# A deformable and a sign convolution on one core: the products of a tap that are added to older weights go in turn to two buffers

## The chip, the cores and the metric

One core of one Trainium2 chip. The metric is the device time of one launch in microseconds. The kernel before took 3805.28 us (median of 3 runs, 3805.22 to 3807.43). A separate, profiled execution took 3809.51 us; its profile spans 3807.5 us.

## The reference

The input `x` is 8 images of 64 x 64 pixels and 256 channels, float32. Two layers follow:

```python
x = x + L0(_gn(x))   # DCNv4: deformable, 32 groups of 8 channels, 9 taps
x = x + L1(_gn(x))   # convolution of signs, 3 x 3, scaled by means of sizes
```

Layer 0 takes the normalised image through a depthwise 3 x 3 convolution and a matmul; that gives, for each pixel, group and tap, an offset (y, x) and a mask. The value image (another matmul) is sampled at the tap's place plus the offset, by bilinear weights, multiplied by the mask and summed over the 9 taps:

```python
sampled = ((1 - ty) * (1 - tx))[..., None] * v00 + ((1 - ty) * tx)[..., None] * v01 \
        + (ty * (1 - tx))[..., None] * v10 + (ty * tx)[..., None] * v11
out = jnp.einsum('nhwgkc,nhwgk->nhwgc', sampled, mask).reshape(n, h, w, c)
return out @ op_w
```

## The kernel before, in words

**Layer 0** (`layer0`) goes through 32 steps: 8 images, and in each image 4 steps `j` = 0 to 3. A step holds 4 rows in each of 4 quarters of the image; partitions are 4 quarters x 32 groups, and the free dimension of a tile is `TOK` = 256 pixels. Image 0 and image 7 are written out, the six between them are one hardware loop, and each step is the same list of work for every engine with small additions: `j` = 2 makes the means and scales of the next image (not for the last image), `j` = 3 prepares two groups of value rows for the next image, the very last step prepares nothing.

Offsets reach less than one pixel, so each tap touches a 3 x 3 set of neighbours, and all nine taps together 5 x 5 = 25 shifts. A step therefore builds `wsum`, the weight of each of the 25 shifts (25 x 256 numbers per partition), and then multiplies the value image, shifted, by each weight and sums the 25 products.

The loop that every engine follows is over the taps `k` = 0 to 8:

- **PE** (`step`, from L838 on): `offsets` of tap k + 2 (L782) in three parts into `ps_om`, between them the first `add` of a product (L830: 16 matmuls with the identity, which turn a `pv` buffer and add it into `ps_add`), then the step's other work: `depthwise` (L753) at taps 0 to 3, `values` (L766) at 4, 5, 7, 8, `turn_back` (L795) at tap 4, `project` (L808) at taps 5 and 6; then the other adds of the tap.
- **ACT**: `hats` of tap k + 2 (L602 to L616: bilinear weights `hat` and mask `msk` from `ps_om`; it waits until the products of tap k are done, for `hat` has two buffers), then it empties PE's banks. At tap 4 (`BACK_AT`) `summed` (L623) copies the finished sums of the previous step from `ps_add` to `acc`; it stands ahead of the `hats` of tap 6 in ACT's list. `keep_back` (L631) then copies what PE turned to `acc_t`.
- **DVE** (`step`, from L1090 on): `products` of tap k (L1009), `multiply` (L1059: one shift's product over 8 channels, 128 x 2048, into one of the 4 buffers of `pv`), `add_products`, `mask_rows` for tap k + 1 (L995), and more `multiply`. There are 25 of these in a step; taps 4 and 5 have two each, the others three.
- **POOL** issues the accumulating DMAs.

Of the 9 products (3 x 3) of a tap, those at shifts that no earlier tap has touched are written to `wsum` itself; the older ones (4 or 6 planes of 256, in one or two rectangles, `tap_rects`) are first written to a buffer, `prod`, and then added to `wsum`. For taps 1, 2, 3, 6 and 7 (`SENT_TAPS`) POOL sends them by a DMA that adds (`add_products` of POOL, L479; its landing raises `wsum_added`), one after another, each behind the landing of the one before. For taps 4, 5 and 8 DVE adds them itself (L1037, `wadd_done`). Since there is one `prod`, DVE's products of tap k wait until the older ones of tap k - 1 have been added:

```python
if k > 0 and k - 1 in SENT_TAPS:
    dve.wait_ge(wsum_added, 16 * (sent_before(TAPS) * s + sent_before(k)))
```

A `multiply` waits for the landing of the last tap that touches its shift (`last_tap`), and for PE's `add` of the product that lay in its `pv` buffer before, four shifts earlier. Shift 0 is not added by PE: POOL adds it to shift 1 by a DMA (`add_pair`).

`acc` (2048 numbers per partition, as `prod`) holds the turned-out sums of the previous step from ACT's `summed` at tap 4 until PE has turned them back (`turn_back`, unit `back3`). Under the name `ahead[0]` it serves a second time: in steps `j` = 0 and 1 POOL loads half of a channel block of the next image there (`load_ahead`, L462) once `back3` is through, and ACT sums it at tap 7 (`sums_ahead`, `sums_made`).

**Layer 1** (`layer1`) is a 3 x 3 convolution of signs with its own statistics; it begins when all of layer 0 is stored and shares nothing with it but the engines.

Of the kernel before, what the change touches and what calls it, by code (L numbers as in the profile page):

```python
# [8 lines left out]
ALU = mybir.AluOpType  # L9
# [115 lines left out]
def sent_before(k):  # L125

    return sum(len(tap_rects(i // 3, i % 3)[1]) for i in SENT_TAPS if i < k)
# [75 lines left out]
def layer0(nc, x, zeros, w_dram, x2, consts, tables, mv2, reach, NI):  # L203


    with ExitStack() as ctx:
# [80 lines left out]
        ROOT_AT = 5  # L287
        BACK_AT, PROJECT_AT = 4, [5, 5, 6, 6]
        AHEAD_AT = 7

        def steps_of_images(eng, step):

# [43 lines left out]
            lo = QR * q + SR * j - 2  # L336
            return max(0, -lo), WR - max(0, lo + WR - H)

        def in_prod(rect):

            a, b, c, d = rect
            at = 6 * TOK if a == 2 and d - c == 2 else 0
            return prod[:, at:at + (b - a) * (d - c) * TOK].rearrange("p (a b t) -> p a b t", a=b - a, b=d - c)

        with nc.Block() as block:
            @block.sync
# [106 lines left out]
            @block.gpsimd  # L453
            def _(pool):
                def load_ahead(n, j, half, used):

                    src = x_v[n + 1][:, j].rearrange("p r w -> p (r w)")
                    if (n, j) != (0, 0):
                        pool.wait_ge(bg_full, unit(n, j, used, NI) + 1)
                    else:  # L460
                        pool.wait_ge(bg_full, unit(n, j, "dw3", NI) + 1)
                    nc.gpsimd.dma_start(ahead[half], src[:, HW // 2 * half:HW // 2 * (half + 1)]).then_inc(x_ahead[half], 16)  # L462

                def add_residual(n, j, units):

                    pool.wait_ge(bg_free, units)
                    for q in range(Q):
                        r0 = QR * q + SR * j
                        nc.gpsimd.dma_start(xres[:, :, q, :].rearrange("p h (r w) -> p h r w", w=W),
                                            x_v[n][:, :, r0:r0 + SR, :], accum_op=ALU.add).then_inc(xres_added, 16)  # L470

                def add_products(n, j, k):

                    s = STEPS * n + j
                    ky, kx = k // 3, k % 3
                    pool.wait_ge(prod_done, TAPS * s + k + 1)
                    at_least(pool, wsum_added, 16 * (sent_before(TAPS) * s + sent_before(k)))
                    for a, b, c, d in tap_rects(ky, kx)[1]:
                        nc.gpsimd.dma_start(wsum[:, ky + a:ky + b, kx + c:kx + d, :], in_prod((a, b, c, d)), accum_op=ALU.add)\  # L479
                            .then_inc(wsum_added, 16)  # L480

                def add_pair(n, j, uv):

                    s = STEPS * n + j
                    pool.wait_ge(pv_full, SHIFTS * s + uv + 1)
                    at_least(pool, pair_added, 16 * (len(PAIRS) * s + PAIRS.index(uv)))
                    nc.gpsimd.dma_start(pv[:, (j + uv) % PBUF, :, :], pv[:, (j + PAIRED[uv]) % PBUF, :, :],
                                        accum_op=ALU.add).then_inc(pair_added, 16)

                for n in range(NI):  # L490
                    for j in range(STEPS):
                        for k in SENT_TAPS:
                            if k == 6:
                                add_pair(n, j, 1)
                                if j < CH and n < NI - 1:
                                    load_ahead(n, j, 0, "back3")
                            add_products(n, j, k)
                        if j < CH and n < NI - 1:
                            load_ahead(n, j, 1, "project3")
                        if (n, j) != (0, 0):  # L500
                            add_residual(*previous(n, j), unit(n, j, "project3", NI) + 1)
# [15 lines left out]
            def _(act):  # L517
# [164 lines left out]
                def step(n, j, first, last):  # L682
                    s = STEPS * n + j
                    n1, j1 = following(n, j)
                    n2, j2 = following(n1, j1)
                    more = not (isinstance(n, int) and n == NI - 1 and j >= STEPS - 2)

                    def place(name):
                        return unit(n, j, name, NI), bank(n, j, name, NI)

                    for k in range(TAPS):
                        if k in MEANS_AT and has_means(n, j, NI):
                            keep_mean(n, j, MEANS_AT.index(k))
                        if k == ROOT_AT and has_means(n, j, NI):
                            act.wait_ge(gx_step, GX_STEPS * n + 11)
                            nc.scalar.activation(var1[:, :], var1[:, :], ACT.Sqrt).then_inc(gx_root, 1)
                        if k == BACK_AT and not first:
                            summed(s - 1)
                        if k + 2 < TAPS:
                            hats(n, j, k + 2)  # L700
                        elif not last:
                            hats(n1, j1, k + 2 - TAPS)
                        if k in DW_AT and not last:
                            u = DW_AT.index(k)
                            if first:
                                for i in shares(FIRST_VALUES, u, DW_UNITS):
                                    keep_values(0, i, *place(f"first{i}"), 1)
                            keep_depthwise(j1, u, *place(f"dw{u}"))
                        if k in VALUES_AT and not last:
                            for i in shares(value_units(j1), VALUES_AT.index(k), len(VALUES_AT)):  # L710
                                keep_values(j1, i, *place(f"value{i}"), 2 * n1 + (1 if j1 == 0 else 2))
                        if k == BACK_AT and not first:
                            for u in range(BACK_UNITS):
                                keep_back(u, *place(f"back{u}"))
                        if k in PROJECT_AT and not first:
                            for u in range(PJ_UNITS):
                                if PROJECT_AT[u] == k:
                                    keep_x2(s - 1, u, *place(f"project{u}"))
                        if k in DW_AT[1:3] and not last:
                            normalise_tri(n1, j1, 1, (DW_AT.index(k) - 1,))  # L720
                        if k == 3 and not last:
                            normalise(n1, j1, 0)
                        if k == 6 and not last and j1 == 0:
                            normalise(n1, j1, 1)
                        if k == AHEAD_AT and j < CH and has_next(n):
                            sums_ahead(n, j, 0)
                        if k == 0 and j in (1, 2) and has_next(n):
                            sums_ahead(n, j - 1, 1)
                        if k == 8 and more:
                            keep_scales(n2, j2)  # L730
                            normalise_tri(n2, j2, 0, (0, 1))
# [176 lines left out]
            def _(dve):  # L908
# [90 lines left out]
                def products(n, j, k):  # L999
# [11 lines left out]
                            mwy[:, a:b, :].unsqueeze(2).to_broadcast(shape), ALU.mult)  # L1011

                    dve.wait_ge(mwy_done, TAPS * s + k + 1)
                    if k > 0 and k - 1 in SENT_TAPS:
                        dve.wait_ge(wsum_added, 16 * (sent_before(TAPS) * s + sent_before(k)))
                    elif k > 1:
                        dve.wait_ge(wadd_done, (TAPS - 1 - len(SENT_TAPS)) * s + kept_before(k))
                    at_least(dve, pv_full, SHIFTS * (s - 1) + (13, 14, 15, 18, 19, 20, 23, 24, 25)[k])
                    for rect in old:
                        product(in_prod(rect), rect)  # L1020
                    for a, b, c, d in new:
                        ins = product(wsum[:, ky + a:ky + b, kx + c:kx + d, :], (a, b, c, d))
                    ins.then_inc(prod_done, 1)
# [1 line left out]
                def kept_before(k):  # L1025
                    return sum(1 for i in range(1, k) if i not in SENT_TAPS)

                def add_products(n, j, k):

                    s = STEPS * n + j  # L1030
                    ky, kx = k // 3, k % 3
                    dve.wait_ge(prod_done, TAPS * s + k + 1)
                    if k == 0 or k in SENT_TAPS:
                        return
                    for a, b, c, d in tap_rects(ky, kx)[1]:
                        w = wsum[:, ky + a:ky + b, kx + c:kx + d, :]
                        ins = nc.vector.tensor_tensor(w, w, in_prod((a, b, c, d)), ALU.add)  # L1037
                    ins.then_inc(wadd_done, 1)

                def multiply(n, j, uv):  # L1040
# [891 lines left out]
```

## Time and profile before

| | |
|---|---|
| median of 3 runs | 3805.28 us (3805.22 to 3807.43) |
| profiled execution | 3809.51 us, span 3807.5 us |
| layer 0, its 32 steps of products | 56 to 3302 us |
| layer 1 | from about 3350 us to the end |
| PE, DVE, ACT, POOL busy | 94%, 90%, 63%, 16% of the span |
| mean granted TensorE clock | 0.987 |
| DMA | 503.88 MB moved, mean 132 GB/s |

PE is the matmul side of TensorE and PEld its weight loads; DVE is VectorE. In the lists of waits, "A <- B" is idle time of A's engine just before A which B's instruction ended. In the lists in order of time the columns are start, duration (both us), engine, line, operation, tiles and count; a bracket gives the idle time before and who ended it. The ends of matmuls are modelled. A step lasts about 102 us; it is counted here from DVE's products of tap 0, which are the only ones of 2304 numbers.

### The profile page before, as it was taken

How to read it: one execution, taken by the hardware profiler on the slowest of the kernel's cores; microseconds unless marked ns; L12 is line 12 of the kernel's file. 1: busy time of each engine (PE TensorE's matmuls, PEld its weight loads, DVE VectorE, ACT ScalarE, POOL GpSimd, SP SyncE). 2: the span in 40 equal slices, each digit the busy share in tenths (PEclk: the TensorE clock that was granted, in tenths of full speed). 3: DMA queues.
4: the chain of work that ended last, by engine and by line, in shares of the span. 5: the costliest groups of instructions: out<-in, count | busy, mean ns of one | idle time of the engine just before them, and what ended most of it. 6: DMA issues, size and time to landing. Idle time of an engine off the chain costs nothing. (4 is left out here: it accounts for less than half of the span.)

```text
span 3807.5 us, 89724 instructions
## 1 busy us (share of the span) xinstructions
PE 3566.0 (94%) x37184; PEld 2312.6 (61%) x37184; DVE 3440.4 (90%) x2659; ACT 2395.1 (63%) x4673; POOL 593.5 (16%) x444
## 2 busy tenths in 40 slices
PE   4899999999999999999999999999999999858998
PEld 2566666666666666666666666666666666623333
DVE  4899999999999899999999999999999999948876
ACT  5676666666776667667666667667766665235554
POOL 0011111110111111111111110111111111104444
PEclk9999999999999999999999999999999999979999
DMA  7455566555655566556655655656655554345553
GB/s 175 115 126 113 125 135 144 121 119 126 140 129 115 125 141 135 106 115 140 135 119 123 141 128 121 128 130 132 135 122 118 115 110 93 58 160 212 210 214 145
DMA packets 324548, 503.88 MB, mean 132 GB/s; under 512 B 37756, under 2 KB 243196, under 8 KB 314248
## 3 DMA queue, kind: packets, MB, share of 16 engines
q0 software_dynamic: 98688, 229.66, 32.7%
q1 hardware_dynamic: 224584, 266.07, 23.3%
q8 instruction: 294, 4.82, 0.5%
q10 hardware_dynamic: 832, 2.10, 0.1%
q14 instruction: 150, 1.23, 0.1%
HBM read 262.53 MB, written 67.41 MB: 87 GB/s over the span
## 5 line engine op out<-in xcount | busy, mean ns | idle before, releaser
L1059 DVE TENSOR_TENSOR pv<-val,wsum 128x2048 f32<-128x2048 f32 x800 | 1809.9, 2287 | 43.3 <-PE ps_add L830 28.6
L830 PEld LDWEIGHTS ps_add<-ident,pv 128*128 128x128 f32 x12288 | 1342.7, 142 | 317.3 <-issue 163.2
L830 PE MATMUL ps_add<-ident,pv 128*128 128x128 f32 x12288 | 1456.7, 275 | 46.2 <-DVE pv L1059 44.7
L782 PE MATMUL ps_om<-xdw,omw 128*32 128x256 f32 x13824 | 867.9, 384 | 69.9 <-ACT hat L604 68.9
L1009 DVE TENSOR_TENSOR prod<-hat,mwy 128x1536 f32<-128x1536 f32 (+1 forms) x384 | 526.3, 1399 | 122.6 <-DMA wsum<-prod 98.4
L782 PEld LDWEIGHTS ps_om<-xdw,omw 128*32 128x32 f32 x13824 | 391.3, 109 | 378.7 <-ACT hat L604 91.8
L479 POOL DMA_DIRECT2D wsum<-prod x192 | 226.2, 1253 | 2255.8 <-DVE wsum L1009 2255.8
L602 ACT ACTIVATE hat<-ps_om,omb 128x256 f32<-128x256 f32 x576 | 275.0, 477 | 452.8 <-PE ps_om L782 437.8
L606 ACT ACTIVATE msk<-ps_om,omb 128x256 f32<-128x256 f32 x288 | 136.5, 474 | 365.4 <-PE ps_om L782 360.2
L753 PE MATMUL ps_bg<-tri,diag 128*32 128x512 f32 x3024 | 346.6, 592 | 12.0 <-ACT tri L568 12.0
L557 ACT ACTIVATE tri<-tri,gn_tri 96x1024 f32<-96x1024 f32 (+1 forms) x376 | 329.8, 950 | 4.7 <-ACT gn_tri L525 4.4
L995 DVE TENSOR_TENSOR mwy<-hat,msk 128x768 f32<-128x768 f32 x288 | 274.6, 953 | 50.4 <-ACT hat L616 50.4
L766 PE MATMUL ps_bg<-win,vpw 128*32 128x256 f32 x4992 | 294.9, 381 | 0.0
L604 ACT ACTIVATE hat<-ps_om,omb 128x256 f32<-128x256 f32 x576 | 280.8, 488 | 0.0
L603 ACT ACTIVATE hat<-ps_om,nomb 128x256 f32<-128x256 f32 x576 | 276.0, 479 | 0.0
L1009 DVE TENSOR_TENSOR wsum<-hat,mwy 128x768 f32<-128x768 f32 (+2 forms) x288 | 257.6, 895 | 2.7 <-DVE pv L1059 1.3
L808 PE MATMUL ps_bg<-acc_t,opw 128*128 128x512 f32 x512 | 240.3, 610 | 1.8 <-ACT val L590 0.8
L766 PEld LDWEIGHTS ps_bg<-win,vpw 128*32 128x32 f32 x4992 | 162.9, 111 | 109.6 <-issue 3.6
L1037 DVE TENSOR_TENSOR wsum<-wsum,prod 128x1536 f32<-128x1536 f32 x192 | 226.1, 1220 | 0.0
L1759 POOL TENSOR_TENSOR c_x<-c_x,c_res 128x1024 f32<-128x1024 f32 x64 | 170.5, 2666 | 340.8 <-ACT c_res L1643 340.8
L753 PEld LDWEIGHTS ps_bg<-tri,diag 128*32 128x32 f32 x3024 | 98.8, 111 | 185.0 <-issue 163.7
L1712 PE MATMUL ps_p<-c_over,c_kw 128*128 128x512 bf16 x768 | 189.3, 397 | 20.1 <-ACT c_res L1637 20.1
(145 smaller groups left out, 2703.7 us busy)
## 6 DMA issues: line engine op xcount, KB each, us to landing
wsum<-prod POOLq DMA_DIRECT2D x160, 768.0 KB, 6.8
tri<-in_x_dram SPq DMA_DIRECT2D x725, 128.0 KB, 2.8
win<-in_x_dram SPq DMA_DIRECT2D x144, 256.0 KB, 3.3
pv<-pv POOLq DMA_DIRECT2D x32, 1024.0 KB, 7.6
x<-xres SPq DMA_DIRECT2D x128, 256.0 KB, 5.5
xres<-in_x_dram POOLq DMA_DIRECT2D x124, 256.0 KB, 9.6
out_dram<-c_x SPq DMA_DIRECT2D x31, 1024.0 KB, 4.8
c_x<-x SPq DMA_DIRECT2D x30, 1024.0 KB, 5.3
```

What stands on the lines that cost most here:

```text
L557: last = nc.scalar.activation(v, v, ACT.Identity, bias=gn_tri[0:KROWS, j % 2, 2 * c + 1, h:h + 1], scale=gn_tri[0:KROWS, j % 2, 2 * c, h:h ...
L602: nc.scalar.activation(hat[:, par, a, 1, :], d, ACT.Abs, bias=b).then_inc(abs_done, 1)
L603: nc.scalar.activation(hat[:, par, a, 0, :], d, ACT.Relu, bias=nb, scale=-1.0)
L604: nc.scalar.activation(hat[:, par, a, 2, :], d, ACT.Relu, bias=b).then_inc(om_free, 1)
L753: mm = nc.tensor.matmul(out[:, :, :, o0:o1], diag[:, h, c, kx, :], src, start=kx == 1, stop=kx == 2)
L766: mm = nc.tensor.matmul(ps_bg[G * q:G * q + G, par, ci * TOK:(ci + 1) * TOK], vpw[:, h, 2 * cp + ci, :], win_of(n, j, i // V_UNITS)[:, h, ...
L782: mm = nc.tensor.matmul(ps_om[G * q:G * q + G, (par + i) % 2, 0:TOK], omw[:, h, comp, :], xdw[:, j % 2, h, q, :], start=h == 0, stop=h == ...
L808: mm = nc.tensor.matmul(ps_bg[:, par, :], opw[:, h, P * oh:P * oh + P], acc_t[:, h, 512 * tb:512 * tb + 512], start=h == 0, stop=h == CH - 1)
L830: mm = nc.tensor.matmul(ps_add[:, tb, c, :], pv[:, (j + uv) % PBUF, c, P * tb:P * tb + P], consts["ident"][:, :], start=uv == ADDED[0] and ...
L995: nc.vector.tensor_tensor(mwy[:, :, :], hat[:, par, 1, :, :], msk[:, par, :].unsqueeze(1).to_broadcast([P, 3, TOK]), ALU.mult)\
L1009: return nc.vector.tensor_tensor(dst, hat[:, par, 0, c:d, :].unsqueeze(1).to_broadcast(shape), mwy[:, a:b, :].unsqueeze(2).to_broadcast(sh ...
L1059: nc.vector.tensor_tensor(pv[:, (j + uv) % PBUF, :, :].rearrange("p c (r w) -> p c r w", w=W), val[:, :, SR * j + u:SR * j + u + SR, v:v + ...
```

## The change

DVE's older products of taps 1 and 3 go to `acc` in every step; in steps `j` = 2 and 3 (`NO_AHEAD`) those of taps 6 and 8 too. All others stay in `prod`. DVE's products of a tap now wait for the last tap that used the same buffer: for its landing if it was sent, for DVE's own add if it was kept. At tap 1 they wait for the `back3` of the step before and, in steps 1 and 2, for ACT's sums over the same buffer; at tap 6 in steps 2 and 3 for the `back3` of the same step. ACT waits at tap 4, ahead of `summed`, for the landing of tap 3. DVE's `add_products` waits for the landings of the sent taps before it, which its products used to wait for. The order of work on each engine stays as it was.

```diff
+        NO_AHEAD = (2, 3)
...
+        def in_acc(j, k):
+            return k in ((1, 3, 6, 8) if j in NO_AHEAD else (1, 3))
+
-        def in_prod(rect):
+        def in_prod(rect, j, k):
...
-            return prod[:, at:at + (b - a) * (d - c) * TOK].rearrange("p (a b t) -> p a b t", a=b - a, b=d - c)
+            return (ahead[0] if in_acc(j, k) else prod)[:, at:at + (b - a) * (d - c) * TOK].rearrange("p (a b t) -> p a b t", a=b - a, b=d - c)
...
                         if k == BACK_AT and not first:
+                            act.wait_ge(wsum_added, 16 * (sent_before(TAPS) * s + sent_before(4)))
                             summed(s - 1)
...
                     dve.wait_ge(mwy_done, TAPS * s + k + 1)
-                    if k > 0 and k - 1 in SENT_TAPS:
-                        dve.wait_ge(wsum_added, 16 * (sent_before(TAPS) * s + sent_before(k)))
+                    same = [i for i in range(1, k) if in_acc(j, i) == in_acc(j, k)]
+                    if k == 1:
+                        if not is_step(n, j, 0, 0) and not is_step(n, j, 0, 1):
+                            dve.wait_ge(bg_free, unit(*previous(n, j), "back3", NI) + 1)
+                        if j in (1, 2) and has_next(n):
+                            dve.wait_ge(sums_made, CH * CH * n + CH * j - 1)
+                    elif k == 6 and in_acc(j, k):
+                        dve.wait_ge(bg_free, unit(n, j, "back3", NI) + 1)
+                    elif k > 1 and same and same[-1] in SENT_TAPS:
+                        dve.wait_ge(wsum_added, 16 * (sent_before(TAPS) * s + sent_before(same[-1] + 1)))
+                    elif k > 1 and same:
+                        dve.wait_ge(wadd_done, (TAPS - 1 - len(SENT_TAPS)) * s + kept_before(same[-1] + 1))
                     elif k > 1:
-                        dve.wait_ge(wadd_done, (TAPS - 1 - len(SENT_TAPS)) * s + kept_before(k))
+                        at_least(dve, wadd_done, (TAPS - 1 - len(SENT_TAPS)) * s)
...
                     if k == 0 or k in SENT_TAPS:
                         return
+                    dve.wait_ge(wsum_added, 16 * (sent_before(TAPS) * s + sent_before(k)))
```

## Rows read from the trace of the kernel before

**Rows 1.** The page, part 1: busy time, share of the span, instructions.
```profile
PE 3566.0 (94%) x37184; PEld 2312.6 (61%) x37184; DVE 3440.4 (90%) x2659; ACT 2395.1 (63%) x4673; POOL 593.5 (16%) x444
```

**Rows 2.** Waits of DVE, 200 to 3200 us: total, times, longest.
```profile
DVE prod L1009 <- DMA wsum<-prod: 96.4, 66, 3.0
DVE pv L1059 <- PE ps_add L830: 28.6, 13, 3.6
DVE prod L1009 <- issue: 17.9, 14, 2.1
```

**Rows 3.** DVE in order of time, taps 1 to 3 of one step.
```profile
1190.77 0.95 DVE L1009 TENSOR_TENSOR wsum<-hat,mwy 128x768 f32<-128x768 f32 x1
...
1200.78 1.76 DVE L1009 TENSOR_TENSOR prod<-hat,mwy 128x1536 f32<-128x1536 f32 x1 [1.59 <-DMA wsum<-prod]
...
1213.87 1.76 DVE L1009 TENSOR_TENSOR prod<-hat,mwy 128x1536 f32<-128x1536 f32 x1 [2.99 <-DMA wsum<-prod]
```

**Rows 4.** Stretches, one image's four steps: length; PE, PEld, DVE, ACT, POOL busy.
```profile
1281.42:1384.57 103.15, 101.31 (x1156) 68.47 (x1154) 95.81 (x67) 67.96 (x139) 14.00 (x13) 1.00 0.60 134
1384.57:1484.51 99.94, 96.89 (x1076) 65.83 (x1072) 96.41 (x70) 69.64 (x138) 14.01 (x13) 1.00 0.62 138
1484.51:1585.87 101.36, 98.14 (x1088) 67.22 (x1085) 97.50 (x79) 68.21 (x142) 12.88 (x11) 1.00 0.56 114
1585.87:1688.01 102.14, 98.77 (x1119) 66.65 (x1121) 95.80 (x67) 67.33 (x137) 12.84 (x11) 1.00 0.57 124
```

**Rows 5.** Waits of PE, 200 to 3200 us: total, times, longest.
```profile
PE ps_om L782 <- ACT hat L604: 47.8, 45, 1.4
PE ps_add L830 <- DVE pv L1059: 21.7, 35, 2.1
PE ps_bg L795 <- ACT val L583: 11.3, 30, 0.4
PE ps_bg L795 <- ACT acc_t L631: 6.1, 30, 0.2
```

**Rows 6.** PE in order of time, tap 4 of one step.
```profile
1224.20 3.71 PE L830 MATMUL ps_add<-ident,pv 128*128 128x128 f32 x32
1227.85 1.93 PE L782 MATMUL ps_om<-xdw,omw 128*32 128x256 f32 x32
1231.04 1.07 PE L782 MATMUL ps_om<-xdw,omw 128*32 128x256 f32 x16 [1.26 <-ACT hat L604]
```

**Rows 7.** DVE in order of time: tap 8 (j = 1), tap 6 (j = 3).
```profile
655.80 2.36 DVE L1009 TENSOR_TENSOR prod<-hat,mwy 128x1536 f32<-128x1536 f32 x2 [2.60 <-DMA wsum<-prod]
...
1252.58 4.49 DVE L1059 TENSOR_TENSOR pv<-val,wsum 128x2048 f32<-128x2048 f32 x2 [2.69 <-PE ps_add L830]
```

**Rows 8.** DVE in order of time, in the last two steps.
```profile
3179.07 4.50 DVE L1059 TENSOR_TENSOR pv<-val,wsum 128x2048 f32<-128x2048 f32 x2
...
3195.77 2.36 DVE L1009 TENSOR_TENSOR prod<-hat,mwy 128x1536 f32<-128x1536 f32 x2 [2.13 <-issue]
...
3293.25 2.36 DVE L1009 TENSOR_TENSOR prod<-hat,mwy 128x1536 f32<-128x1536 f32 x2 [1.41 <-issue]
```

**Rows 9.** PE in order of time, in the last two steps.
```profile
3177.05 3.66 PE L830 MATMUL ps_add<-ident,pv 128*128 128x128 f32 x32
...
3225.80 1.97 PE L830 MATMUL ps_add<-ident,pv 128*128 128x128 f32 x16 [2.68 <-DVE pv L1059]
...
3266.23 3.68 PE L830 MATMUL ps_add<-ident,pv 128*128 128x128 f32 x16 [3.35 <-DVE pv L1059]
```

**Rows 10.** ACT in order of time, tap 4 of one step (j = 1).
```profile
1433.30 1.94 ACT L623 ACTIVATE acc<-ps_add 128x1024 f32<-128x1024 f32 x2 [0.65 <-PE ps_add L830]
...
1442.17 0.60 ACT L631 ACTIVATE acc_t<-ps_bg 128x512 f32<-128x512 f32 x1 [0.26 <-PE ps_bg L795]
```

**Rows 11.** POOL in order of time: the DMA of tap 3, same step.
```profile
1422.15 1.20 POOL L479 DMA_DIRECT2D wsum<-prod  x1 [10.06 <-DVE wsum L1009]
```

**Rows 12.** DMA issues, 160 to 3200 us: KB each, median us to landing.
```profile
wsum<-prod POOLq DMA_DIRECT2D x150, 768.0 KB, 6.9
```

More of the change, by code:

```diff
@@ L478, in add_products @@
                     for a, b, c, d in tap_rects(ky, kx)[1]:
-                        nc.gpsimd.dma_start(wsum[:, ky + a:ky + b, kx + c:kx + d, :], in_prod((a, b, c, d)), accum_op=ALU.add)\
+                        nc.gpsimd.dma_start(wsum[:, ky + a:ky + b, kx + c:kx + d, :], in_prod((a, b, c, d), j, k), accum_op=ALU.add)\
                             .then_inc(wsum_added, 16)
@@ L1013, in products @@
                     dve.wait_ge(mwy_done, TAPS * s + k + 1)
-                    if k > 0 and k - 1 in SENT_TAPS:
-                        dve.wait_ge(wsum_added, 16 * (sent_before(TAPS) * s + sent_before(k)))
+                    same = [i for i in range(1, k) if in_acc(j, i) == in_acc(j, k)]
[10 more added lines that the diff above has]
+                        dve.wait_ge(wadd_done, (TAPS - 1 - len(SENT_TAPS)) * s + kept_before(same[-1] + 1))
                     elif k > 1:
-                        dve.wait_ge(wadd_done, (TAPS - 1 - len(SENT_TAPS)) * s + kept_before(k))
+                        at_least(dve, wadd_done, (TAPS - 1 - len(SENT_TAPS)) * s)
                     at_least(dve, pv_full, SHIFTS * (s - 1) + (13, 14, 15, 18, 19, 20, 23, 24, 25)[k])
                     for rect in old:
-                        product(in_prod(rect), rect)
+                        product(in_prod(rect, j, k), rect)
                     for a, b, c, d in new:
@@ L1034, in add_products @@
                         return
+                    dve.wait_ge(wsum_added, 16 * (sent_before(TAPS) * s + sent_before(k)))
                     for a, b, c, d in tap_rects(ky, kx)[1]:
                         w = wsum[:, ky + a:ky + b, kx + c:kx + d, :]
-                        ins = nc.vector.tensor_tensor(w, w, in_prod((a, b, c, d)), ALU.add)
+                        ins = nc.vector.tensor_tensor(w, w, in_prod((a, b, c, d), j, k), ALU.add)
                     ins.then_inc(wadd_done, 1)
```

## The prediction

> **What bounds the kernel now.** I read the page first, then who waits for whom, then busy time by stretch, then the order of time where waits sit. The page shows PE and DVE nearly full together [rows 1], so busy shares alone choose neither. Layer 0 is 32 steps, four per image, of about 102 us; layer 1 begins near 3350 us and is not touched.
>
> In the steady stretch (200 to 3200 us) DVE waits 96.4 us before L1009 for the DMA that adds `prod` into `wsum`, in 66 places, and another 17.9 us in 14 places where no releaser is given but which stand at the same spots; it waits 28.6 us for PE, to get a `pv` buffer back [rows 2]. The first two sum to 114.3 us, and they are what the edit aims at. In order of time one sees the cause: DVE finishes tap 1's products at 1191.7 (1190.77 + 0.95), has 7.5 us of other work (a mask and three `pv` products), and then stands 1.59 us; tap 2's products take 2.6 us, and after them it stands 2.99 us [rows 3]. So from the products' end to the landing it took 9.1 us (1200.78 less 1191.7) and 10.5 us (1213.87 less 1203.4).
>
> But a wait of DVE is paid for only if PE stands too. One image's four steps: PE is busy 101.31 of 103.15 us, 96.89 of 99.94, 98.14 of 101.36, 98.77 of 102.14 [rows 4]. In the first, DVE stood 7.34 us (103.15 less 95.81) and PE only 1.84: DVE's lateness was covered by the four `pv` buffers. **PE sets the pace.** All its waits in the steady stretch are 47.8 us for ACT's `hat`, 21.7 for DVE's `pv`, 11.3 + 6.1 for ACT's copies [rows 5]. Of the 47.8, 30 waits are the same one, 1.26 us each, once per step at tap 4 (ACT copies `ps_add` out before it frees `ps_om`) [rows 6]; it hangs on PE and ACT alone. That is 37.8 us; the other 15 waits, 10.0 us, come from late products, since L602 waits for `prod_done`. So what DVE's lateness costs PE is 10.0 + 21.7 = **31.7 us**, not 114.
>
> **The change, part by part.**
> (a) Waits removed. With taps 1 and 3 in `acc` and 2 and 4 in `prod`, tap 2 needs no landing, taps 3 and 4 wait for the DMA of two taps before. DVE's pitch per tap is some 10.1 us of its own work (2.6 for products plus 7.5), against 9.1 and 10.5 us from products to landing, with another tap added on top: covered. Taps 7 and 8 are freed only in steps 2 and 3 of an image; in steps 0 and 1 tap 8 keeps its wait (1.41 to 2.60 us in rows of such waits [rows 7, 8]). For DVE this removes about 114.3 less some 15 kept waits of 1.9 = 85 us; for PE at most 31.7.
>
> (b) Is all 31.7 removed? In steps 3 and 0 DVE already runs as far ahead as the buffers let it: at tap 6 it waits 2.69 us for PE's add [rows 7]. From such a lead steps 0 and 1 run with no wait of PE on `pv`. In step 1, DVE now keeps its lead; step 2 has the next image's scales in it and DVE is busy 97.5 us instead of 95.8 to 96.4 [rows 4], and it begins behind tap 8's kept wait. There I leave PE 0.4 to 0.5 us per image, 3 us in all. 31.7 less 3 = 28.7 us.
>
> (c) The last step has no next one to prepare, so DVE sets its pace: PE waits 2.68 and 3.35 us for `pv` there [rows 9]. On the way to it two landing waits fall away, 2.13 at tap 8 of the step before and 1.41 at its own [rows 8]. At tap 6 of the step before, DVE is already at the limit of its lead (its product begins at 3179.07 [rows 8], and the add that frees that buffer is the first half of PE's 3.66 us from 3177.05 [rows 9]), so nothing more is carried in. Gain 3.5 us.
>
> (d) The first step: DVE is fed by PE and ACT, has no landing wait at taps 2 to 4 and keeps that of tap 8. Zero.
>
> (e) Waits added. Tap 1 on DVE now waits for the previous `back3` and in steps 1 and 2 for ACT's sums over `acc`; both are over with ACT's tap 7 of the step before, two taps or 20 us earlier. Zero. Tap 6 in steps 2 and 3 waits for `back3` of its own step: in step 1 of the image shown ACT's last copy to `acc_t` begins at 1442.17 and takes 0.6 [rows 10]; DVE's tap 6 is at 65 us of a step, that is near 1449, so 6 us of cover. In step 3, where DVE had 2.69 us of waiting ahead of it to give up and some 3 us come free, 1 to 2 us are left. If the cover went, DVE would stand while PE still has all of tap 5 (some 10 us) before it needs a product of tap 6: nothing is lost until DVE is later than that. `add_products` now waits for tap 3's landing at tap 4 behind one product set and one `pv` (2.6 + 2.2 us later than the old wait stood): zero.
> (f) ACT's `summed` now waits for the DMA of tap 3 too. Behind it in ACT's queue stand the `hat` of tap 6, and PE behind those. POOL issues that DMA at 1422.15 [rows 11] and it lands a median of 6.9 us later [rows 12], near 1429; `summed` begins at 1433.30 [rows 10]. Cover 4 us; the serial chain of three DMAs at a 10.2 us pitch can slip about 1. I take zero, since a wait already met delays nothing; as the upper bound I take the smallest hand-over between engines in the rows, ACT's `acc_t` to PE, 6.1 us in 30 waits or 0.2 us each [rows 5]: 31 x 0.2 = 6 us. Below zero is excluded, a wait gains nothing.
> No byte of traffic and no arithmetic is added; POOL's order is the same.
>
> **Sum.** 28.7 + 3.5 = 32 us. The profiled execution took 3809.5, so 3777 for it; it stood 4.2 above the median of 3805.3, and from the median it is **3773 us**, 0.8% less. Bounds of the known terms: 31.7 + 3.5 + 1.5 for the second step's start gives 37 (3768); half of PE's 31.7 kept gives 16 + 3.5 = 19 (3786); the 6 us of (f) give 3779.
>
> **Rivals.**
> 1. *DVE sets the pace and PE only looks full.* For: DVE is 90% busy and its waits are the longest. Against: the step in which DVE lost 7 us and PE 1.8. If it held, all 85 + 3 us would come: 3717. Of the rule in the Trainium skill (Perfetto Trace Analysis, Identifying the Most-Contended Engine) that matmul busy share says little of TensorE's headroom and weight-load busy share says more: by weight loads, 2312.6 us or 61% [rows 1], PE would have much to spare, which is this rival. The trace disagrees: PE's blocks of 32 matmuls follow one another without a gap (3.71 us from 1224.20, the next at 1227.85 [rows 6]). Chance 0.04.
> 2. *Nothing measurable.* The waits go from DVE's L1009 to DVE's L1059 for `ps_add`, and PE's own waits stay, for they come from some other order (mask and `hat`, the pair's DMA). For: DVE already shows 28.6 us of waits for PE. Against: PE's `pv` waits sit just after DVE's landing waits. Within 5 us: 3800 to 3805. A page would lead here: the Trainium skill (DMA: Bandwidth & Descriptors, Anatomy of one DMA) gives 2.0 us plus bytes over 436 GB/s, an estimate of 3.8 us for 768 KB, and then DVE's 7.6 us would cover every landing. The trace does not agree: 6.9 us [rows 12]. Chance 0.08.
> 3. *Half.* DVE's lead in steps 1 and 2 is eaten by tap 8's kept wait and the scales, so PE keeps half its waits: 3786 to 3794. Chance 0.15.
> 4. *Slower.* Tap 3's DMA lands after PE's last add, so `summed` holds ACT, the `hat` of tap 6 and PE. Its place is tap 4 of 31 steps. It decides once landing comes over 4 us later than now; with three DMAs stacked and 8 us late it would cost 31 x 4 = 124, less 32: near 3895; if it just overruns by 1.5 us, 3820. Against it: the chain's pitch. Chance 0.05.
>
> **How the numbers follow.** The forecast has 0.68. A measurement of this kernel tells 0.2% (7.6 us) from no change. Faster: forecast, half, rival 1: 0.68 + 0.15 + 0.04 = 0.87. Within: 0.08. Slower: 0.05. The range takes the forecast's bounds, widened by 2 below for the end of the lead I can't see, and half of case 3: 3766 to 3790.
>
> **What would show it.** In the changed profile: DVE's waits for the `wsum` DMA down to some 15 of 1.9 us, all at tap 8 of steps 0 and 1; DVE's waits for `ps_add` up to about 80 us, in nearly every step at tap 6; PE's waits for `pv` near 3 us and for `hat` near 38 in 30 places of 1.26; PE idle 1.8 to 2.3 us in every step; steps of 99.5 to 101.5 us. ACT at L623 released by PE, never by the DMA. The forecast is wrong if PE's 1.26 us wait grows, if PE's matmul blocks themselves lengthen, or if DVE is released at L1059 by something other than PE.

## The result and the profile after

The changed kernel took 3784.1 us (median of 4 runs, 3783.97 to 3784.41), the one before 3806.4 beside it: 22.3 us less, a ratio of 0.9939 (95% interval 0.9922 to 0.9956). In a second comparison, with its own runs of the kernel before, it was 3784.2 against 3807.3, 0.9933 (0.9919 to 0.9946). The forecast was 3773, range 3766 to 3790: the direction and the range held, the gain was 0.7 of the one forecast. The profiled execution spans 3782.2 us, 25.3 less than the one of before.

The waits of DVE and of PE, 200 to 3175 us (total, times, longest), which answer to [rows 2] and [rows 5]:

```profile
DVE pv L1075 <- PE ps_add L835: 80.6, 24, 6.4
DVE prod L1014 <- DMA wsum<-prod: 27.2, 12, 2.6
DVE mwy L1000 <- ACT hat L620: 9.1, 15, 0.9
DVE prod L1014 <- issue: 4.9, 3, 2.2
```

```profile
PE ps_om L787 <- ACT hat L608: 51.5, 45, 1.4
PE ps_bg L800 <- ACT val L587: 11.3, 30, 0.4
PE ps_bg L800 <- ACT acc_t L635: 6.1, 30, 0.2
PE ps_add L835 <- DVE pv L1075: 2.8, 8, 0.5
```

DVE's waits for landings fell from 114.3 to 32.1 us in 15 places (27.2 + 4.9), its waits for PE rose from 28.6 to 80.6: the wait moved to the ring of four `pv` buffers. PE's waits for `pv` fell from 21.7 to 2.8. PE's waits for `hat`, of which 10.0 us were to go, rose from 47.8 to 51.5.

The four steps of one image by stretch (length; PE, PEld, DVE, ACT, POOL busy), which answer to [rows 4]:

```profile
1270.88:1374.98 104.10, 102.26 (x1164) 69.77 (x1167) 95.96 (x67) 68.95 (x142) 14.00 (x13) 1.00 0.63 133
1374.98:1473.44 98.46, 96.47 (x1074) 65.69 (x1070) 96.30 (x71) 69.37 (x138) 14.01 (x13) 1.00 0.63 140
1473.44:1572.31 98.87, 96.45 (x1072) 66.08 (x1068) 97.41 (x80) 66.69 (x139) 12.87 (x11) 1.00 0.57 117
1572.31:1674.70 102.39, 98.99 (x1134) 66.42 (x1127) 95.62 (x67) 68.05 (x139) 12.85 (x11) 1.00 0.57 123
```

The image takes 403.8 us instead of 406.6. Steps are counted from DVE's work, and DVE's lead over PE changes from step to step, so the first and last got longer while 1 and 2 got 1.5 and 2.5 us shorter; only the sum tells something. Steps 1 and 2 now hold DVE 98% and 99% busy, steps 0 and 3 have it wait 4.25 and 6.39 us for PE.

Counted by PE, at the first matmul of its turn-back, the 25.3 us come off in these places:

| from, to | before | after | less |
|---|---|---|---|
| start, tap 4 of step 1 | 218.35 | 217.30 | 1.05 |
| tap 4 of step 1, tap 4 of step 30 | 2945.70 | 2927.17 | 18.53 |
| tap 4 of step 30, last turn-back | 171.65 | 167.91 | 3.74 |
| last turn-back, layer 1's first matmul | 25.59 | 23.17 | 2.42 |
| layer 1 | 446.20 | 446.62 | -0.42 |

The fourth row can't be put down to the change. In it lies the last projection, 16 matmuls. It took 8.98 us in the kernel before, at a mean granted clock of 0.79, and 7.13 us in the changed one, at 1.00; in the second profile of the changed kernel (`e9_after_again`, below) the stretch took 26.04 us and the projection 9.30, at 0.76. All profiles of this study show the projection either at 7.13 us or at 8.9 to 9.6. The rows, with length, PE busy and its count, clock, DMA share and GB/s:

```profile
3339.70 8.98 PE L808 MATMUL ps_bg<-acc_t,opw 128*128 128x512 f32 x16 [0.69 <-ACT acc_t L631]
3339.70:3348.68 8.98, 8.97 (x16) 0.79 0.00 1
```

```profile
3315.57:3322.70 7.13, 7.13 (x16) 1.00 0.00 0
```

### The profile page after: what moved, and what is told of

It is laid out like the page before. It is cut to its first block and busy times, and to the rows that moved or that the text cites. A ratio compares the mean times of both kernels' runs of the same rounds, so it can differ in the third digit from the quotient of the medians.

```text
span 3782.2 us, 89899 instructions
## 1 busy us (share of the span) xinstructions
PE 3557.5 (94%) x37184; PEld 2308.1 (61%) x37184; DVE 3437.6 (91%) x2659; ACT 2394.9 (63%) x4673; POOL 593.5 (16%) x444
## 5 line engine op out<-in xcount | busy, mean ns | idle before, releaser
L835 PE MATMUL ps_add<-ident,pv 128*128 128x128 f32 x12288 | 1453.7, 275 | 24.3 <-DVE pv L1075 23.6
L1014 DVE TENSOR_TENSOR prod<-hat,mwy 128x1536 f32<-128x1536 f32 (+1 forms) x272 | 347.6, 1311 | 38.0 <-DMA wsum<-prod 28.8
L483 POOL DMA_DIRECT2D wsum<-acc x80 | 98.5, 1232 | 1417.5 <-DVE wsum L1014 1398.8
L483 POOL DMA_DIRECT2D wsum<-prod x112 | 127.6, 1269 | 785.8 <-DVE wsum L1014 785.8
```

What stands on the lines that cost most here:

```text
L835: mm = nc.tensor.matmul(ps_add[:, tb, c, :], pv[:, (j + uv) % PBUF, c, P * tb:P * tb + P], consts["ident"][:, :], start=uv == ADDED[0] and ...
L1014: return nc.vector.tensor_tensor(dst, hat[:, par, 0, c:d, :].unsqueeze(1).to_broadcast(shape), mwy[:, a:b, :].unsqueeze(2).to_broadcast(sh ...
```

## The experiments

Each is compared with runs of the kernel before on its own chip; that median was 3809.7 us for the first four, 3809.1 for the next four, 3807.3 for the last four. Compare ratios, or differences from before. The two values of the last projection (see above) can put 2 to 3 us into a time, so smaller differences of two medians mean little; and the kernel before varies most, from 3803.8 to 3817.0 us in all. The steady stretch alone, from PE's turn-back at tap 4 of step 1 to the one of step 30, in the one profile of each (us; that of the last row was the fastest of its eleven runs):

| kernel | steady stretch |
|---|---|
| before; with ACT's wait alone | 2945.7; 2945.8 |
| changed; the same again | 2927.2; 2926.4 |
| only taps 1 and 3; only taps 6 and 8 | 2928.1; 2940.3 |
| changed, `tri` cut in two in all steps | 2931.2 |
| DVE relieved, after; before | 2923.0; 2921.6 |
| changed, PE relieved | 2914.9 |
| changed, all of `summed` behind | 2960.7 |
| changed, half of the copy behind; and `tri` cut in two | 2920.1; 2908.0 |
| before, with both edits of ACT's list | 2938.3 |

### Only taps 1 and 3

```diff
-        NO_AHEAD = (2, 3)
+        NO_AHEAD = ()
```

> The changed kernel with NO_AHEAD empty: only taps 1 and 3 go to acc, so DVE waits for the landings of taps 6 and 7 in every step. Theory P (PE sets the pace, and DVE's lateness costs only where PE then stands): PE's waits for pv and hat at the start of steps 2 and 3 (some 1.4 us and 1.8 us an image in the kernel before) stay partly, the one at tap 3 goes; between the two kernels, 3790 to 3797 against 3784 and 3806. Theory D (DVE sets the pace): DVE's landing waits fall from 114 to about 57 us, so half of the way in any case, and the same fraction of DVE's removed waits should come off the time.

3790.0 us, 0.9945 (0.9932 to 0.9959): 19.7 less than before.

### Only taps 6 and 8

```diff
-            return k in ((1, 3, 6, 8) if j in NO_AHEAD else (1, 3))
+            return j in NO_AHEAD and k in (6, 8)
...
-                    if k == 1:
...
-                    elif k == 6 and in_acc(j, k):
+                    if k == 6 and in_acc(j, k):
...
-                            act.wait_ge(wsum_added, 16 * (sent_before(TAPS) * s + sent_before(4)))
```

> Only taps 6 and 8 of steps 2 and 3 go to acc; taps 1 and 3 stay in prod, and ACT's new wait is left out. Theory P: the waits at taps 2 to 4 of step 0 cost nothing (PE stood only 1.84 us there), the wait at tap 3 of step 1 still costs up to 1.5 us of PE an image, the ones at the starts of steps 2 and 3 mostly go: 3790 to 3797. Theory D: DVE loses about 30 us of its 114 us of waits, a quarter of what the change removes: 3798 to 3800.

3797.0 us, 0.9966 (0.9954 to 0.9978): 12.7 less. Together the parts would give 32.4 us, and both at once give 22 to 23. So they overlap, though less than these numbers say: in the steady stretch the parts take off 17.6 and 5.4 us, both at once 18.5. Taps 1 and 3 alone give nearly all of it. Theory P put both runs at 3790 to 3797, where their times lie; but its numbers were counted from 3806, and the first run's 19.7 us under its own runs of before are more than the 9 to 16 that P allowed. Theory D, by DVE's waits removed, wanted the second 6 to 8 us off before, not 12.7, and the first half way, not 19.7.

### ACT's new wait alone

```diff
+                            act.wait_ge(wsum_added, 16 * (sent_before(TAPS) * s + sent_before(4)))
                             summed(s - 1)
```

> The kernel before with ACT's new wait for tap 3's landing ahead of summed, and nothing else. Theory P: tap 3 has landed about 4 us earlier, no change, within 2 us of before. Theory W (the 10 us missing from the forecast were lost in the new wait): 6 to 10 us slower than before, 3812 to 3816.

3810.0 us, 1.0000 (0.9991 to 1.0009). Theory P's range was hit: the wait costs nothing that these runs can tell. In its trace ACT's copy is released by PE in all 30 places, 15.0 us in total against 14.6 in the kernel before:

```profile
ACT acc L623 <- PE ps_add L831: 15.0, 30, 0.7
```

### ACT's scaling of `tri` cut in two

The remaining candidate was the 13.7 us of `hat` waits of PE beyond the 30 of 1.26. In the changed kernel's trace they stand at the start of steps 2 (0.57 us) and 3 (1.40 us). PE, then ACT, in order of time, at the start of step 3:

```profile
1579.12 1.96 PE L835 MATMUL ps_add<-ident,pv 128*128 128x128 f32 x16
1582.50 1.07 PE L787 MATMUL ps_om<-xdw,omw 128*32 128x256 f32 x16 [1.41 <-ACT hat L608]
```

```profile
1574.62 1.07 ACT L594 ACTIVATE val<-val 32x1024 f32<-32x1024 f32 x1
...
1576.21 4.65 ACT L561 ACTIVATE tri<-tri,gn_tri 96x1024 f32<-96x1024 f32 x4 [0.18 <-ACT gn_tri L529]
1580.96 0.42 ACT L572 ACTIVATE tri<-tri 32x256 f32<-32x256 f32 x1
1581.28 0.45 ACT L606 ACTIVATE hat<-ps_om,omb 128x256 f32<-128x256 f32 x1
```

ACT is busy for 6.7 us ahead of that `hat`, with a break of 0.18, and all of it is its own work of tap 8. No product is late: DVE's products of tap 0, which this `hat` must wait for, ended at 1574.87 (1572.31 + 2.56). The experiment moves half of the scaling:

```diff
+                        if k == 0 and not first and not last:
+                            normalise_tri(n1, j1, 0, (1,))
...
-                            normalise_tri(n2, j2, 0, (0, 1))
+                            normalise_tri(n2, j2, 0, (0,))
```

> The changed kernel with ACT's scaling of tri at tap 8 cut in two: the first two quarters at tap 8, the other two after the depthwise copy at tap 0 of the next step, where PE needs them one tap later. Theory A (the waits of PE for hat at the start of steps 2 and 3, 0.57 and 1.40 us in the changed kernel, are ACT's own 5 us of work ahead of the hat, not DVE's lateness, and are what the forecast of 10.0 us was wrong about): both waits go, 2.0 us an image, 13 to 15 us in all, 3769 to 3771. Theory K (the missing 10 us are tap 8's kept landing waits in steps 0 and 1): no change, 3784.

3791.2 us, 0.9953 (0.9939 to 0.9966): outside both ranges, no gain, if anything a loss against the changed kernel. But the trace shows both waits of 0.57 and 1.40 us gone, and others in their place one tap later, up to 1.36 us in step 1 and 1.91 in step 2: there ACT also sums half an image over `acc_t` at tap 0 (`sums_ahead`), and the moved half, 2.9 us, pushes the next `hat` behind it. Theory A was right on whose work it is and wrong on the price.

### DVE relieved, after and before

```diff
-                        ins = nc.vector.tensor_tensor(w, w, in_prod((a, b, c, d), j, k), ALU.add)
+                        ins = nc.vector.tensor_tensor(w[:, 0:1, 0:1, 0:1], w[:, 0:1, 0:1, 0:1], in_prod((a, b, c, d), j, k)[:, 0:1, 0:1, 0:1], ALU.add)
```

> The changed kernel with DVE's own adds of taps 4, 5 and 8 cut to one number each (this part of the sum is left out): some 6.7 us less DVE work per step, 210 us in all. Theory P (PE sets the pace): PE's pv waits of 2.8 us go, the first and the last step, where DVE sets the pace, give some 6 us each: 3768 to 3776. Theory D (DVE sets the pace): near 3580.

> The same cut in the kernel before, whose 114 us of landing waits stay. Theory P: DVE's lateness vanishes by its lead, PE's pv waits of 21.7 us go although every landing wait stays, and the time ends beside the run with the cut in the changed kernel, 3768 to 3780. Theory D: 210 us less, near 3600, and the changed kernel with the cut some 80 us below it.

After: 3767.5 us, 0.9887 (0.9872 to 0.9903). Before: 3771.0 us, 0.9894 (0.9879 to 0.9909). Some 210 us less work of DVE take 38 us off the kernel before and, by the ratios, 18 to 20 off the changed one, and bring both to nearly one time. Of the latter only 4 us lie in the steady stretch; 6 come off ahead of it and 8 behind it, in the first and last steps, where PE in the changed kernel stands for `pv` again and again (3.29 us at tap 5 of the last). In the second, DVE's landing waits are all there, even a little longer, and PE's `pv` waits are gone; its waits of DVE and of PE:

```profile
DVE pv L1059 <- PE ps_add L830: 128.4, 35, 6.4
DVE prod L1009 <- DMA wsum<-prod: 106.9, 84, 3.2
...
DVE prod L1009 <- issue: 17.5, 17, 1.9
```

```profile
PE ps_om L782 <- ACT hat L604: 49.6, 45, 1.4
...
PE ps_add L830 <- DVE pv L1059: 0.4, 1, 0.4
```

124 us of landing waits (106.9 + 17.5) with only 0.4 us of PE's waits for `pv` beside them: such waits cost nothing while DVE has lead enough, and theory D, which wanted 3580 and 3600, has fallen. And the `hat` waits are 49.6 us with DVE far ahead, so the 10.0 us were never its lateness.

### PE relieved

```diff
-                        for c in range(GC):
+                        for c in range(GC // 2 if uv in (12, 18) else GC):
```

> The changed kernel with half of PE's matmuls left out in the adds of shifts 12 and 18 (that part of the sum is left out): 16 matmuls of 0.116 us per step, 1.86 us, 59 us in all. Theory P: PE gives it back almost whole until DVE limits, whose own work and kept waits are near 390 us an image against PE's 396 after the cut: 50 to 59 us, 3725 to 3735. Theory D: no change.

3773.7 us, 0.9909 (0.9894 to 0.9924): about 11 us against the changed kernel (12 in the steady stretch), where 50 to 59 were expected by theory P and none by theory D. PE has 59 us less to do and stands instead:

```profile
PE ps_om L787 <- ACT hat L608: 70.3, 58, 2.3
PE ps_add L835 <- DVE pv L1075: 18.9, 33, 1.4
```

Against the changed kernel that is 18.8 us more for `hat` and 16.1 more for `pv`. The waits at the start of steps 2 and 3 are 1.45 and 2.28 us in most images, 0.9 longer each, which is the whole of the half add cut at tap 8: there ACT's work of tap 8 sets the time and PE only fills it. The clock's part is small: it fell once in 160 to 3150 us, for 3.4 us. Theory P, as I had it, has fallen too. I read it so that no one engine sets the pace: in the steps of the changed kernel shown above PE stands 1.8 to 3.4 us, in steps 1 and 2 DVE no more than 1.5 to 2.2, and at single taps PE waits for ACT's list. Which of them holds which tap was not shown for the rest of the step.

### All of `summed` behind the first half of the `hat`

```diff
                         nc.scalar.activation(hat[:, par, a, 2, :], d, ACT.Relu, bias=b).then_inc(om_free, 1)
+                        if a == 0 and between:
+                            between()
...
-                        if k == BACK_AT and not first:
+                        def sums_out():
                             act.wait_ge(wsum_added, 16 * (sent_before(TAPS) * s + sent_before(4)))
                             summed(s - 1)
...
-                            hats(n, j, k + 2)
+                            hats(n, j, k + 2, sums_out if k == BACK_AT and not first else None)
```

> The changed kernel with summed moved behind the first half of the hat of tap 6 in ACT's list. Theory P and S (the 1.26 us wait once per step is ACT's 1.94 us of copying ahead of the hat, and PE sets the pace): the wait shrinks to 0.2 us, about 1 us in each of 31 steps, 3750 to 3756. Rival R (PE's turn-back waits for the later copy instead): 3780 to 3786.

3818.9 us, 1.0022 (1.0013 to 1.0031): 9.8 slower than before, by the ratios some 33 slower than the changed kernel, and outside both ranges. The 1.26 us wait did shrink, to 0.46; but ACT now idles until the offsets are there before it copies, everything behind it in its list comes later, and PE stands 1.99 us (0.38 before) ahead of the turn-back. PE in order of time, and the granted clock by stretch (length, PE busy, clock, DMA share, GB/s):

```profile
1342.48 0.66 PE L803 MATMUL ps_bg<-ident,acc 128*128 128x128 f32 x4
1345.13 1.14 PE L803 MATMUL ps_bg<-ident,acc 128*128 128x128 f32 x8 [1.99 <-ACT val L587]
1346.48 1.12 PE L803 MATMUL ps_bg<-ident,acc 128*128 128x128 f32 x4 [0.21 <-ACT acc_t L637]
1347.52 3.08 PE L790 MATMUL ps_om<-xdw,omw 128*32 128x256 f32 x32
```

```profile
1340.00:1345.00 5.00, 3.14 (x52) 1.00 0.92 186
1345.00:1350.00 5.00, 4.66 (x38) 0.66 0.21 33
1350.00:1355.00 5.00, 5.00 (x76) 1.00 0.92 265
```

The granted clock falls to its lower level (half, 1.2 GHz) for some 3.4 us: 32 matmuls of the offsets take 3.08 us instead of 1.93 [rows 6]. Such falls stand in 13 of the steps between 160 and 3150 us, 44.4 us at half speed in all. I estimate from this at most 22 us lost (half of 44.4); in the same stretch the kernels before and after have none. So up to two thirds of the 33 us are the clock's, and PE's waits for ACT and DVE, 13 us longer than in the changed kernel, make about the rest.

### The last four, on one chip

The changed kernel again was the base.

> The changed kernel once more, on the chip of the three runs that follow, as their base: 3784 to 3788, PE idle in a steady step 1.84, 1.9, 2.4 and 3.25 us.

3784.2 us, 0.9933 (0.9919 to 0.9946), as expected.

Half of the copy behind:

```diff
-                            summed(s - 1)
+                            summed(s - 1, (0,))
...
-                            hats(n, j, k + 2)
+                            hats(n, j, k + 2, (lambda: summed(s - 1, (1,))) if k == BACK_AT and not first else None)
```

> The changed kernel with only the first of summed's two copies ahead of the hat of tap 6, the second behind its first half. ACT's list has no added idle time ahead of the value copy, unlike the run with all of summed behind. Theory C (the pace is the loop of PE and ACT, and the 1.26 us wait hangs on ACT's copies ahead of the hat): the wait falls by one copy, 0.97 us, to 0.3; 31 steps, 30 us; turn-back waits stay at 0.38; the granted clock shows no dips to a half: 3754 to 3760. Rival (DVE or another wait takes it, as when PE's matmuls were cut): 3775 to 3784.

3778.7 us, 0.9919 (0.9905 to 0.9932): 5.6 less than its base, where theory C expected 30; the rival's range, 3775 to 3784, was hit. No run of it is as slow as the fastest of its base. Its waits of PE:

```profile
PE ps_om L791 <- ACT hat L608: 27.9, 46, 1.4
PE ps_bg L804 <- ACT val L587: 27.0, 30, 1.1
```

`hat` 23.6 us less, of the 30 expected, but the turn-back 15.7 us more: PE arrives 0.8 us earlier at the next thing that ACT must have done, the copy of the values, and ACT's list ahead of that is as long as it was. No fall of the clock in 160 to 3150 us.

The same, and `tri` cut in two only ahead of step 3:

```diff
+                        if k == 0 and j == STEPS - 1 and not last:
+                            normalise_tri(n1, j1, 0, (1,))
...
-                            normalise_tri(n2, j2, 0, (0, 1))
+                            normalise_tri(n2, j2, 0, (0,) if j2 == 0 else (0, 1))
```

> The last run's kernel, and in addition the scaling of tri at ACT's tap 8 cut in two only where the next step has no sums over acc_t at tap 0 (step 3 next). Theory A (PE's 1.40 us wait for hat at the start of step 3 is ACT's own work and moves nowhere, since tap 0 of that step has room): 1.4 us an image less, 8 to 10 us below the last run, 3745 to 3751. Rival (DVE, idle only 1 to 2 us in steps 1 and 2, now sets the pace): no more than 3 us.

3765.4 us, 0.9884 (0.9869 to 0.9899): 13.3 less than the last, where theory A had put 8 to 10 (and 3745 to 3751 in all, for it built on the 30 us of the last run); 18.8 less than the changed kernel, 41.9 less than before. **The fastest kernel of the study that computes the whole.** PE's waits:

```profile
PE ps_bg L806 <- ACT val L587: 27.0, 30, 1.1
PE ps_om L793 <- ACT hat L608: 16.3, 38, 0.5
PE ps_bg L806 <- ACT acc_t L639: 6.0, 30, 0.2
PE ps_add L841 <- DVE pv L1081: 3.3, 7, 0.6
```

In step 3, tap 0 has no `sums_ahead`, and there the 1.4 us go and come back nowhere: `hat` 11.6 us less.

Both edits of ACT's list in the kernel before:

> The kernel before with the same two edits of ACT's list and one prod. Theory L (one prod costs DVE's lateness beyond what the loop of PE and ACT leaves it): with that loop about 1 us a step faster, most of the 114 us of landing waits lies open; the gain is eaten in steps 1 to 3 and the distance to the last run's kernel grows from 23 to 40 or 50 us, 3785 to 3798. Rival (the two buffers are worth a fixed 23 us): 3768 to 3774.

3804.3 us, 0.9994 (0.9985 to 1.0003). Not to be told from no change, and slower than both theories' ranges. The distance to the same kernel with two buffers is 38.9 us, near the 40 to 50 of theory L and far from the fixed 23 of the rival. Here PE's waits for `pv` are the ones that grew, from 21.7 to 29.8 us:

```profile
PE ps_add L836 <- DVE pv L1065: 29.8, 44, 1.6
PE ps_bg L801 <- ACT val L583: 25.9, 29, 1.1
PE ps_om L788 <- ACT hat L604: 15.8, 37, 0.5
```

## Why the forecast was right in its direction and short in its size

- **Waits removed, (a).** Right: 82.2 us of DVE's landing waits went (85 forecast), 15 of them stayed, at tap 8 of steps 0 and 1 (1.9 to 2.6 us each in the images of the loop), and they came back as waits for `ps_add`, 80.6 us (80 forecast). The place was half right: they were to stand in nearly every step, and they stand in steps 0 and 3, 4.25 and 6.39 us; in steps 1 and 2 of the images of the loop DVE never reached the end of its lead.
- **What of it PE had paid, (b).** The `pv` part was right: 21.7 us to 2.8 (3 left forecast), 18.9 gained. The failed step is the other term: "the other 15 waits, 10.0 us, come from late products, since L602 waits for `prod_done`". They come from ACT's own list: 4.65 us of scaling `tri` and more ahead of the `hat` of tap 2. The code has that `prod_done` wait, but it was met. The sign could be read before: the waits stood only at the start of steps 2 and 3, where ACT has that scaling behind it, and in step 2 they had the same length, 0.29 or 0.30 us, in every image of the loop; in step 3 they were 1.21 to 1.42 us but for two of 0.77 and 0.72, ahead of which PE had just stood 0.6 us for `pv`. With PE on time they are 0.57 to 0.59 and 1.39 to 1.41 us in the images of the loop; all of PE's waits for `hat` together grew by 3.7 us. So PE's waits fell by 15.2 us in the steady stretch, not by 28.7. Two signs that the prediction named came out otherwise with it: PE stands 1.84, 1.99, 2.42 and 3.40 us in the four steps, not 1.8 to 2.3 in each, and its waits for `hat` did not fall to 38 us.
- **The steady stretch.** It got 18.5 us shorter, counted by PE. PE's idle time in it fell by 16.1 us (87.2 to 71.2), of which the 15.2 are the waits named. For the other 2.4 us PE is busy less, with the same 32016 matmuls and the same mean length of every group; where they come from stays open.
- **The last steps, (c).** Forecast 3.5 us, and 3.7 came between tap 4 of step 30 and the last turn-back. Part of that can be the clock, which was at its lower level for 10.2 us there in the profile before and for 6.8 in the one after. PE's `pv` wait at tap 5 of the last step is 3.29 us, as it was (3.35); the one of 2.68 fell to 0.44.
- **The first step, (d).** 1.1 us came off there (step 1 begins at 164.56 instead of 165.67), not zero. DVE waits there for a landing at tap 8 in both traces, 2.07 us before and 1.56 after; the rest was not looked into.
- **Behind layer 0's products.** 2.4 us of the 25.3 came off there, 1.9 of them in the last projection at its two granted clocks. No term had this, and the changed kernel shows both values; it is luck of the profiled execution.
- **Waits added, (e) and (f).** Zero each, as said; (f) by its own experiment. The wait of tap 6 for `back3` shows only where DVE was relieved (13.0 us in 8 places), and in that run PE has no wait for `pv` in the steady stretch.
- **What bounds the kernel.** "PE sets the pace" gave the right account of this change, for it counted PE's own waits. As a rule for the kernel it was wrong: 59 us less work of PE gave 11.
- **Rivals.** 1 (DVE sets the pace) fell with the relieved DVE. 2 and 4 did not come. 3 (half) is nearest to what came in size, but its reason was wrong: DVE kept its lead. The sentence of the Trainium skill under rival 1 (Perfetto Trace Analysis, Identifying the Most-Contended Engine), that weight-load busy share says more of TensorE's headroom than matmul busy share, these runs bear out in part: at 94% of matmul and 61% of weight-load busy time PE did not set the pace alone, for relieved of 59 us it gave back 11. But DVE, with 90% the fullest engine by that way of counting, gave back no more than 20 of 210. The skill's estimate under rival 2 (DMA: Bandwidth & Descriptors, Anatomy of one DMA), 3.8 us to landing, stays apart from what was measured: 6.7 us from `prod` and 7.2 from `acc` in the page of the changed kernel.

## What to carry to other kernels

When three engines pass work in a ring and none has much to spare, a removed wait is worth only what the next engine's list leaves: read for each wait of the slowest engine what its releaser was doing in the 10 us before, not only which semaphores it might have waited on. The worth of one fix depends on the others: the second buffer gave 23 us with ACT's list as it was and 39 with ACT's list shortened, and ACT's shorter list gave 3 us without the buffer, which is not to be told from none, and 19 with it. Work of a side engine is best moved to the tap where it has room, and in this kernel that differs by step: the split that won 13 us in one step of four gave nothing when made in all (there without the half copy; the split in one step was not tried without it). And before a few us are put down to a change, see where in the profile they came off: here 2.4 of 25.3 came off where the change does nothing.

## What was not expected of the hardware

A stand of PE of 1.99 us between short transposes, in a kernel that otherwise keeps it 97% busy, was followed by about 3.4 us at the lower granted clock in 13 of the 22 steps that have it, at most 22 us lost; in the other 9 steps, and after the stands of 0.94 us in step 3, it was not. With that stand at 1.1 us (the half copy) no step has such a fall. In the run with PE relieved, stands of 2.1 to 2.3 us ahead of the `hat` of step 3 come seven times, and the clock fell after one of them. So a stand of 2 us can bring a fall and need not; what decides was not tried. The same holds for the last projection, which two profiles of one and the same kernel show at different clocks.
